# Second stage of a two-layer convolution kernel: the next image's TensorE pieces dealt out anew over the half steps, and values made two granules ahead

## The reference, cut to what matters

```
x = x + conv4x4(group_norm_32(x), outer([1,3,3,1],[1,3,3,1])/64)        # the same kernel for each channel
y = group_norm_32(x)
t = relu(group_norm(d4_1x1(y, w1)))                  # 32 x 8 channels
weights = w2 . t + b2                                # 9 taps for each of 4 groups x 8 elements, turned per element
values  = d4_1x1(y, w_v)                             # 512 channels
out = x + sum over 9 taps of weights[tap] * shifted(values, tap)
```

## Time and profile before

| | before |
|---|---|
| median of three runs | 5196.06 us |
| profiled execution | 5190.41 us |
| its span, first to last instruction | 5188.6 us |
| mean granted TensorE clock | 0.961 |
| busy PE / DVE / POOL / ACT | 4650.8 (90%) / 4464.1 (86%) / 3903.4 (75%) / 2864.1 (55%) |
| idle of DVE just before L1149, 512 times | 254.1, of which 252.1 ended by PE's L803 |
| idle of PE just before L801 | 335.3, of which 311.2 ended by DVE's prod_d |

### The profile page before, as it was taken

One profiled execution on the slowest core, in us unless ns is written; L12 is line 12 of the kernel. 1 busy time (PEld: TensorE's weight loads), 2 busy tenths in 40 slices (PEclk: granted clock), 3 DMA queues, 4 the chain that ended last, 5 costly groups with the idle time before them and its releaser, 6 DMA issues.

```text
span 5188.6 us, 117277 instructions
## 1 busy us (share of the span) xinstructions
PE 4650.8 (90%) x39036; PEld 1648.4 (32%) x39036; DVE 4464.1 (86%) x7761; ACT 2864.1 (55%) x4642; POOL 3903.4 (75%) x1952
## 2 busy tenths in 40 slices
PE   8999999978989898988989898989898989898965
PEld 3333333322333232333333232323232323232322
DVE  6777777734989898989899999989898989898998
ACT  7999999955444444444445454444444444444421
POOL 6888888833878787777777787778787868787888
PEclk9999999989999999999999999999999999999987
DMA  8999999943333233333333233333332323332321
GB/s 237 257 257 257 257 256 256 247 107 90 102 102 115 87 113 97 106 99 103 99 103 109 93 111 99 106 95 115 99 111 91 115 91 111 99 116 90 105 71 65
DMA packets 872972, 679.71 MB, mean 131 GB/s; under 512 B 560224, under 2 KB 822752, under 8 KB 856032
## 3 DMA queue, kind: packets, MB, share of 16 engines
q1 hardware_dynamic: 872416, 672.79, 44.2%
HBM read 404.21 MB, written 268.44 MB: 130 GB/s over the span
## 4 chain that ended last, share of the span: by engine, by line
PE 40%; DVE 16%; issue 12%; POOL 7%; ACT 3%; DVEq 0%; POOLq 0%; DMA 0%; SPq 0%; ACTq 0%
PE ps L801 8%; PE ps L748 7%; POOL acc L1054 7%; PE ps L803 6%; PE ps L738 6%; PE ps L789 5%; DVE prod_d L1105 5%; PE ps L776 5%; DVE prod_p L1105 4%; DVE ps L1149 3%; PE ps L763 2%; DVE ps L1105 2%; DVE six_t L1070 1%; DVE acc L1151 1%; ACT xh L901 1%
## 5 line engine op out<-in xcount | busy, mean ns | idle before, releaser
L1054 POOL TENSOR_TENSOR acc<-acc,prod_p 128x1024 f32<-128x1024 f32 x1280 | 3040.7, 2376 | 848.1 <-DVE acc L1151 701.0
L1105 DVE TENSOR_TENSOR prod_p<-ps,val 128x1024 f32<-128x1024 f32 x1280 | 1555.0, 1215 | 39.8 <-issue 27.8
L1105 DVE TENSOR_TENSOR prod_d<-ps,val 128x512 f32<-128x512 f32 x1536 | 1042.6, 680 | 10.7 <-ACT ps L959 10.7
L299 PE MATMUL ps<-xn,band 64*64 64x512 f32 x8192 | 948.0, 598 | 21.4 <-issue 12.9
L801 PE MATMUL ps<-acc,base 128*128 128x512 f32 x1024 | 620.6, 690 | 335.3 <-DVE prod_d L1105 311.2
L748 PE MATMUL ps<-xh,wh 128*32 128x512 f32 x6144 | 729.1, 602 | 70.5 <-ACT xm L909 24.8
L331 POOL TENSOR_TENSOR x_out<-x_out,x_in 128x512 f32<-128x512 f32 x512 | 636.4, 1275 | 0.0
L259 ACT ACTIVATE x_out<-ps 64x512 f32<-64x512 f32 x1024 | 606.2, 592 | 50.4 <-PE ps L299 28.7
L959 ACT ACTIVATE ps<-ps,b 128x256 f32<-128x256 f32 x576 | 236.7, 445 | 664.7 <-PE ps L789 661.4
L803 PE MATMUL ps<-prod_d,base 128*128 128x512 f32 x1024 | 589.4, 661 | 0.0
L776 PE MATMUL ps<-xm,base 128*32 128x256 f32 (+1 forms) x8192 | 574.8, 418 | 2.5 <-ACT xm L933 2.4
(11 more groups left out here) (76 smaller groups left out, 3706.8 us busy)
## 6 DMA issues: line engine op xcount, KB each, us to landing
x_in<-x SPq DMA_DIRECT2D x128, 1024.0 KB, 7.4
x<-x_out SPq DMA_DIRECT2D x256, 512.0 KB, 5.2
xr<-x SPq DMA_DIRECT2D x512, 256.0 KB, 3.4
acc<-x SPq DMA_DIRECT2D x1024, 128.0 KB, 3.1
out<-acc SPq DMA_DIRECT2D x256, 512.0 KB, 2.7
prod_p<-wsrc SPq DMA_DIRECT2D x1, 384.0 KB, 5.3
w<-w2t SPq DMA_DIRECT2D x1, 288.0 KB, 5.1
shift_m<-shifts SPq DMA_DIRECT2D x1, 256.0 KB, 5.7
```

The costliest lines, as they stand in the source:

```text
L299: mm = nc.tensor.matmul(ps[to:to + H2, 2 * two + t, :], band[rows, v, rows], group(xn[rows, k % N_RING, :], XP, W, v, 2 * two + x), start= ...
L1054: nc.gpsimd.tensor_tensor(acc[:, r, :], acc[:, r, :], prod_p[:, k % P_RING, :], ALU.add).then_inc(p_added, 1)
L1105: return nc.vector.tensor_tensor(dst.rearrange("p (m r w) -> p m r w", m=count, w=W), taps_of(tap).rearrange("p (m r w) -> p m r w", m=1, ...
```

## The change

TensorE's pieces for the next image are dealt out anew, ScalarE's keeping and SyncE's loads follow the same tables, values are made two granules ahead in place of three (so the turn from one image to the next makes values of granule 1 alone, not 1 and 2), and the moments of the third strip of t move from granule 11 to granule 13. No operation is added or left out.

```diff
--- before.py
+++ after.py
@@ -62,7 +62,7 @@
 VP = W + 2
 BR = H // BANDS + 2
 ROWS = [6, 4, 4, 4]
-AHEAD = GRANS - 1
+AHEAD = GRANS - 2
 
 
 D_TAPS, P_TAPS = (0, 1, 2, 3), (4, 5, 6, 7, 8)
@@ -79,17 +79,18 @@
 
 
 
-FORWARD_1 = {3: ((2, 1),), 5: ((3, 0),), 7: ((4, 1),), 9: ((5, 0),)}
-FORWARD_2 = {0: ((0, 0), (0, 1)), 1: ((1, 0), (1, 1)), 2: ((2, 0),), 5: ((3, 1),), 6: ((4, 0),), 9: ((5, 1),),
-             10: ((6, 0), (6, 1)), 12: ((7, 0), (7, 1))}
-BLOCK_V_1 = {1: ((0, 0), (0, 1)), 2: ((1, 0),), 6: ((3, 0), (3, 1)), 10: ((5, 0), (5, 1)), 14: ((7, 0), (7, 1))}
-BLOCK_V_2 = {2: ((1, 1),), 4: ((2, 0), (2, 1)), 8: ((4, 0), (4, 1)), 13: ((6, 0), (6, 1))}
-BLOCK_T_1 = {5: (2,), 9: (4,), 13: (7,)}
-BLOCK_T_2 = {1: (0,), 2: (1,), 6: (3,), 10: (5,), 12: (6,)}
-INVERSE_1 = {2: (0,), 3: (1,), 7: (3,), 11: (5,), 13: (6, 7)}
-INVERSE_2 = {5: (2,), 9: (4,)}
-LOAD_AT = {1: 1, 2: 2, 4: 3, 6: 4, 8: 5, 10: 6, 11: 7}
-LOAD_NEXT_AT = 13
+FORWARD_1 = {3: ((2, 1),), 5: ((3, 1),), 7: ((4, 1),), 10: ((6, 0), (6, 1)), 11: ((7, 0), (7, 1))}
+FORWARD_2 = {0: ((0, 0), (0, 1)), 1: ((1, 0), (1, 1)), 2: ((2, 0),), 4: ((3, 0),), 6: ((4, 0),),
+             8: ((5, 0), (5, 1))}
+BLOCK_V_1 = {1: ((0, 0),), 14: ((7, 0), (7, 1))}
+BLOCK_V_2 = {2: ((0, 1),), 4: ((1, 0), (1, 1)), 5: ((2, 0), (2, 1)), 6: ((3, 0), (3, 1)), 9: ((4, 0), (4, 1)),
+             10: ((5, 0), (5, 1)), 13: ((6, 0), (6, 1))}
+BLOCK_T_1 = {1: (0,), 2: (1,), 5: (2,), 6: (3,), 9: (5,), 12: (7,)}
+BLOCK_T_2 = {8: (4,), 10: (6,)}
+INVERSE_1 = {2: (0,), 7: (3,), 13: (7,)}
+INVERSE_2 = {2: (1,), 5: (2,), 9: (4,), 12: (5, 6)}
+LOAD_AT = {1: 1, 2: 2, 4: 3, 6: 4, 8: 5, 9: 6, 10: 7}
+LOAD_NEXT_AT = 12
 MOMENTS_AT, EDGES_AT = 14, 14
 RSTD_AT = (13, 4)
 EDGES = 2
@@ -833,7 +834,6 @@
         variances(0)
         tap_weights(0, 0, EARLY + LATE)
         values(1)
-        values(2)
 
         def half_step(i, n, of_t, of_inverse, of_v, of_forward):
             for c in of_t.get(n, ()):
@@ -985,7 +984,6 @@
         act.wait_ge(const_in, 16 * 6)
         tap_bias(0, 0, EARLY + LATE)
         keep_values(0, 1)
-        keep_values(0, 2)
 
         def keep_half_step(i, n, of_t, of_inverse, of_v, of_forward):
             for c in of_t.get(n, ()):
@@ -1013,7 +1011,6 @@
                         edges(i + 1)
                     if n == N_GRAN - 1:
                         keep_values(i + 1, 1)
-                        keep_values(i + 1, 2)
                         relu(i + 1, 0)
                     if n == MOMENTS_AT:
                         keep_values(i + 1, 0)
@@ -1173,9 +1170,8 @@
                 t_stats(i + 1, 0)
             if more and n == 8:
                 t_stats(i + 1, 1)
-            if more and n == 11:
+            if more and n == 13:
                 t_stats(i + 1, 2)
-            if more and n == 13:
                 t_stats(i + 1, 3)
                 t_aggregate(i + 1)
```

## The result

The changed kernel takes 5148.57 us (median of four runs, 5146.07 to 5152.85) against 5193.48 us before (four runs, 5189.98 to 5196.19): a ratio of 0.9915 with a 95% interval of 0.9898 to 0.9932, 45 us faster. The forecast was 5157 within 5124 to 5196. The profiled execution took 5146.07 us, 44.3 less than that of before. Of these, images 1 to 14 give 35.4 (they begin at 1466.1 and end at 4909.2, a mean of 245.9 for 248.5), image 0 gives 6.7 (247.8 for 254.5), and 2.2 lie in the first stage and in image 15.

A forecast was written before the change was run, and what follows sets the result against it. DVE and PE, both near their limit, hand work over 32 times an image. Waits of 11.3 + 0.4 + 2.6 = 14.3 against 17.5 give images of 246.1; -33, with the start -36, makes 5154, median 5157, range 5124 to 5196.

The forecast's parts named there:

- The carry of half steps: PE's load per half step, its lateness carried through all 32 of an image: 11.3 us of waits against 10.7.
- At full clock worth nothing, or a loss of 0.6: Whole image: without clock effects the new order's waits are 11.3 us against 10.7, so no gain from order.
- 3.0 an image for the stretches of granules 9 and 12: Add_twos slowed after PE idle of about 2.2 us in granules 9 and 12: that cost, 3.0 us an image, goes.
- Idle of 5.8 and 6.9: PE's idle grows to 5.8 us before granule 14 and 6.9 at the turn, costing waits of 0.4 and 2.6.
- An image of 246.1: Image length: waits fall from 17.5 to 14.3 us, so 249.3 - 3.2 = 246.1.
- The start: Granule 0 of image 0: one values piece fewer ahead of it, 2.9 us won.
- only moved: Rival: seven fuller half steps each 0.3 us longer give back 2.1 an image, so no change, 5186; chance 0.17.
- Slower: Rival: clock lowered before granule 14 stays at 1.2 GHz up to the turn, image 253.6, total about 5264; chance 0.13.
- SP's moved loads: Loads asked for in granule 10: they take some 6 us, F7 begins about 10 us later, so no cost.

The follow-up runs named there:

- the filled kernels: b_fill and a_fill2: the kernel before and the changed kernel with matmuls no output needs in PE's idle; 5125.0 and 5119.3 us.
- b_fill912: Kernel before, plus three matmuls no output needs behind the last pieces of granules 8 and 11 each; 5151.9 us, ratio 0.9921.
- a_fill: Changed kernel, plus matmuls no output needs: nine behind granule 13, eleven in the turn's first half step; 5126.8 us, ratio 0.9872.
- a_relu: Changed kernel with ScalarE's relu of granules 1 to 3 moved behind the keeping of the first half step's pieces; 5095.2 us, ratio 0.9815.
- a_fill2: Changed kernel, filled more densely: twelve matmuls no output needs behind granule 13, thirteen at the turn; 5119.3 us, ratio 0.9852.
- b_fill: Kernel before, plus matmuls no output needs: three behind granules 5, 8, 11 and 13 each, six in granule 15; 5125.0 us, ratio 0.9869.

## Why the prediction was right, step by step

- *The carry of half steps* held. Granule 1's second half waits 2.84 (2.9 forecast), granule 11 1.13 and 0.43 (1.25 and 0.5), granule 12 1.18 (1.05), granule 3's second half nothing. Granule 2 was mis-sized: 1.41 for 2.0, in part since F10 and F11 in granule 1 ran in 3.93 and not 4.3. Two of its sums are off: 1.45 + 1.92 + 8.1 - 7.1 is 4.4, not 4.2 to 4.3, and the waits named for the new order add up to 10.55, not 10.9.
- *At full clock worth nothing, or a loss of 0.6*: held in image 1 of the filled kernels, 242.8 and 243.0. Behind a turn the new order wins 0.8, which the forecast did not have.
- *3.0 an image for the stretches of granules 9 and 12*: too high. The clock cost 2.1 there in image 7 and 1.7 on the mean (the table). The mean image of b_fill912 is 245.4 for 248.5, 3.1, but half of what its waits fell by lies at granules 14, 15 and 0, and the profiled execution took 5143.4, where the median is 5151.9. That 1.5 of idle left in granule 9 would not lower the clock held in all 14 images; 1.87 did elsewhere (a_fill).
- *Idle of 5.8 and 6.9*: 5.92 and 6.84. The waits after them came to 0.3 in granule 14 (0.4 forecast), and at the turn to 0.4 in granule 15 and 2.3 and 0.3 in granule 0, 3.0 on the mean of 14 images for the 2.6 forecast.
- *An image of 246.1*: 245.9. L1146's wait was 12.3 in image 7 and 12.6 on the mean, for 14.3. That it came out to 0.2 is partly luck: on the mean, granules 1 to 8 won 3.3 where the terms of the forecast give about 2, granules 9 to 13 lost 0.1 where they give a gain of about 0.5, and the turn won 0.5 where they give 1.2. And 249.3, from which the 3.2 was taken, is image 7's; the mean of before was 248.5.
- *The start* was too small. I gave image 0 only the 2.9 of its first wait, and it won 6.7; of the other 3.8, 3.1 are waits in granules 1 to 5 and 0.2 in granules 9 to 13. These 3.8, 2.4 in images 1 to 14 and 2.2 in the first stage and image 15 are the 8 us by which the profiled execution lies below the 5154 forecast for it.
- *Rivals*: of "only moved" the first half is nearly true, the new order moves waits from granules 1 to 5 into granules 9 to 13 and gains little by it, but the clock's part was won. "Slower" failed at its point of decision: behind granule 14's idle the clock was back by V7 (x32 in 3.71). SP's moved loads cost nothing; no piece F of image 7 waits for its load.

What stays open is why one rest of idle lowers the clock and a like one does not (1.87 and 1.86 above; 2.17 and 2.19; in image 13 of before, 2.20 in granule 9 and 2.26 in granule 12 left the clock at 1.00); no run here varied that alone. It is also open why filling granules 8 and 11 changed how often the clock fell in granules 6, 14 and 0.

## What to carry to other kernels

Where two engines hand work to each other and both are near full, sum the work of each hand-over's stretch, carry the lateness, and price the new order so before it is built; then look at where the idle of the engine falls whose clock drops behind idle, since that can be most of the gain. Where a wait becomes shorter need not be where the gain was made: run both orders with the idle filled before the gain is put down to one of them. A stretch of idle that cannot be used can be filled with work that is thrown away. And before pieces are dealt out anew, look for a stall inside them: here one long activation in front of a ring of two banks cost more than the order and its clock together (53 us, a_relu, against 45).

## What the runs showed that was not expected

Six matmuls of 256 columns an image, thrown away, are worth 39 us of 5191 (b_fill912), and twenty-five bring the changed kernel from 5148.6 to 5119.3 (a_fill2). Each of the loop's 13 turns leaves PE idle, for 2.7 to 3.6 in a_fill2, which no reordering here removed. Where the idle ahead of it is filled, the first add_two behind the turn runs slow in seven (a_fill2) and nine (b_fill) of the 13 images.
